# Reordering the scalar engine, the tail pair and the late stores of a vision-transformer layer with CoPE attention and routed experts

## The reference, cut to what matters

```python
h = concat([cls, patches(x) @ W.T + b]) + pos_embed       # 64 images x 37 tokens x 256
# attention: 16 heads of 64, within each image
q, k, v = h @ Wq, split(h @ Wkv)
sim = q @ k.T * scale
P = reverse_cumsum(sigmoid(sim)); P = minimum(P, 63)      # CoPE positions
E = q @ pos_emb                                           # a table of 64 per row
sim = sim + w * E[ceil(P)] + (1 - w) * E[floor(P)]        # w = P - floor(P)
h = layernorm(h + softmax(sim) @ v @ Wout + b_out)
# feed-forward: router takes 2 of 8 experts per token, plus a shared expert
shared = silu(h @ shared_gate) * (h @ shared_up) @ shared_down
routed = sum over 2 experts e: score_e * (silu(h @ gate_e) * (h @ up_e) @ down_e)
out = layernorm(h + shared + routed)
```

## Time and profile before

| what | value |
| --- | --- |
| runs | 741.5 us median of 3 (740.51 to 741.54) |
| the profiled execution | 741.82 us, its span 740.1 us |
| PE busy | 690.8 us, 93% of the span |
| DVE busy | 489.3 us, 66% |
| ACT busy | 418.5 us, 57% |
| the chain that ended last | PE 79%, SP's queue 7%, DMA 5%, ACT 5% |
| granted TensorE clock, mean | 0.98 of full speed |

### The profile page before, as it was taken

One profiled execution on the slowest core, in us unless ns is written; L12 is line 12 of the kernel. 1 busy time (PEld: TensorE's weight loads), 2 busy tenths in 40 slices (PEclk: granted clock), 3 DMA queues, 4 the chain that ended last, 5 costly groups with the idle time before them and its releaser, 6 DMA issues.

```text
span 740.1 us, 14154 instructions
## 1 busy us (share of the span) xinstructions
PE 690.8 (93%) x4720; PEld 590.9 (80%) x4721; DVE 489.3 (66%) x1027; ACT 418.5 (57%) x730; POOL 122.8 (17%) x156
## 2 busy tenths in 40 slices
PE   8996899999999999999999996969799999999996
PEld 5895696969879696969789693848687999999885
DVE  3374687878978787878879787558582222222667
ACT  1653667576676667566675654532215777775363
POOL 2100000000000000000000000000003777775130
PEclk9998999999999999999999999889899999999999
DMA  8720131515141241414131114048003555552811
GB/s 275 207 64 15 37 72 49 97 49 99 54 93 50 66 83 34 95 51 83 54 65 46 36 43 131 23 117 285 21 1 83 136 141 136 142 139 63 277 66 52
DMA packets 85110, 67.17 MB, mean 91 GB/s; under 512 B 51277, under 2 KB 76347, under 8 KB 85079
## 3 DMA queue, kind: packets, MB, share of 16 engines
q1 hardware_dynamic: 80506, 56.73, 29.6%
q0 software_dynamic: 4224, 9.71, 4.4%
q10 hardware_dynamic: 348, 0.34, 0.1%
HBM read 35.60 MB, written 15.75 MB: 69 GB/s over the span
## 4 chain that ended last, share of the span: by engine, by line
PE 79%; SPq 7%; DMA 5%; ACT 5%; issue 3%; DVE 1%; ACTq 0%; DVEq 0%; POOLq 0%
PE ps_S L920 13%; PE ps_S L1408 10%; PE ps_X L1062 8%; PE ps_X L1014 7%; PE ps_S L999 7%; PE ps_S L1138 6%; PE ps_S L1420 5%; PE ps_S L1053 5%; PE ps_S L911 5%; SPq L637 4%; PE ps_S L1341 4%; PE ps_X L920 2%; PE ps_S L929 2%; PE ps_S L1036 1%; SPq L706 1%
## 5 line engine op out<-in xcount | busy, mean ns | idle before, releaser
L1014 PE MATMUL ps_X<-wkv_sb,hT 128*120 128x512 f32 (+1 forms) x176 | 83.1, 604 | 6.3 <-ACT v_sb L1518 6.3
L1408 PEld LDWEIGHTS ps_S<-attnT,v_sb 128*128 128x128 f32 x704 | 84.7, 192 | 4.9 <-ACT attnT L1748 2.8
L1408 PE MATMUL ps_S<-attnT,v_sb 128*128 128x128 f32 x704 | 85.9, 275 | 1.4 <-ACT attnT L1748 1.4
L1901 DVE COPY_PREDICATED table<-bit,table 111x112 f32<-111x112 int16 (+6 forms) x110 | 74.8, 680 | 11.2
L814 POOL TENSOR_TENSOR rs<-ve,neg_half 111x2 f32<-111x2 f32 x11 | 12.2, 1112 | 414.2 <-DVE ve L1987 414.2
L2332 DVE COPY attnT<-ps_S 128x256 f32<-128x256 f32 x44 | 18.7, 424 | 81.1 <-PE ps_S L1420 80.9
L920 PE MATMUL ps_S<-hT,wq_sb 128*128 128x216 f32 (+1 forms) x320 | 62.5, 347 | 5.2 <-ACT kT L1468 5.2
L1014 PEld LDWEIGHTS ps_X<-wkv_sb,hT 128*120 128x120 f32 (+1 forms) x176 | 28.9, 179 | 43.5 <-issue 28.9
L920 PEld LDWEIGHTS ps_S<-hT,wq_sb 128*128 128x128 f32 x320 | 56.4, 188 | 8.3 <-issue 7.0
L1062 PE MATMUL ps_X<-oT,wout_sb 128*128 128x222 f32 x320 | 62.9, 353 | 0.0
L1062 PEld LDWEIGHTS ps_X<-oT,wout_sb 128*128 128x128 f32 x320 | 59.3, 190 | 1.5 <-issue 1.5
(11 more groups left out here) (321 smaller groups left out, 1332.4 us busy)
## 6 DMA issues: line engine op xcount, KB each, us to landing
down_sb<-in_x_dram SPq DMA_DIRECT2D x10, 648.0 KB
gu_sb<-y_d SPq DMA_DIRECT2D x8, 512.0 KB, 6.6
attnT<-attn SPq DMA_DIRECT2D x126, 28.9 KB
h_d<-hT SPq DMA_DIRECT2D x11, 240.0 KB, 2.5
kept<-h_d SPq DMA_DIRECT2D x11, 240.0 KB, 2.7
h_d<-h SPq DMA_DIRECT2D x10, 222.0 KB
attnT<-attn SPq DMA_DIRECT2D x63, 34.7 KB
wkv_sb<-in_L_attn_Wkv_dram SPq DMA_DIRECT2D x2, 1024.0 KB, 12.4
```

Source lines behind the costliest of these rows:

```text
L1014: mm = nc.tensor.matmul(X[:keyed, 1 - s], hT[:, k].rearrange("p b t -> p (b t)")[:, at:at + keyed], wkv_sb[:, k, INNER + 512 * s:INNER + 5 ...
L1408: mm = nc.tensor.matmul(S[:, i, j * FF + f * P:j * FF + f * P + P], held[:, i, k, j, f * P:f * P + P], xgT[:, i, k], start=(k == 0), stop= ...
L1901: A.did(V.copy_predicated(near[:, :, :, 0:SL - d], by_side(bit[:, n], r)[:, :, :, 0:SL - d], near[:, :, :, d:SL]))
```

## The change

- **ACT in every pair:** `values(p,0,1)` and, where `ahead`, `weights(2p-1)` come before `gates(p,0)`.
- **PE in every pair:** the wait for all keys copied moves from ahead of the queries to ahead of their last quarter.
- **Pair 1:** `outputs(0,0)` comes after `score(1,0)` and `values(1,0,1)` and waits for the copies of that score; the score no longer waits for the output copies.
- **Groups 0, 19 and 20:** of the nine placing transfers SP issues six and ACT three, right after its `weights`.
- **The end pair:** chunks 0 to 3 are turned before `outputs(19,1)`, `distance(20)` comes between their copies; the routes of chunks 6, 2, 4 and `by_half` come before `outputs(20,0)`, as do ACT's `logits_out` and `distance(21)`; PSUM banks of turned and routed chunks change.
- **SP's list at the end:** the halves of pair 9 are stored after the first two expert loads, the down loads come last.

The diff, cut:

```diff
+        def to_diagonal(j, b):
+            n, at = in_block[j], from_slot[j]
+            return own_T[PAD * b:PAD * b + PAD, b, at:at + n], turned_attn[PAD * j:PAD * j + PAD, b, :n]
+        def in_two_queues(g):
+            return isinstance(g, int) and (g == 0 or g >= G - 3)
...
+        ROUTES = (0, FULL - 1, 2, 4)
...
@@ SP, place_attn(p, a) @@
-                for j in range(TPG):
-                    n, at = in_block[j], from_slot[j]
+                for j in range(TPG - in_two_queues(g)):
                     for b in range(TPG):
-                        sp.dma_start(own_T[...], turned_attn[...]).then_inc(placed[a], 16)
+                        sp.dma_start(*to_diagonal(j, b)).then_inc(placed[a], 16)
...
@@ SP, end of its list @@
             for t in range(KE):
                 for j, w in enumerate((gate_w, up_w)):
                     sp.dma_start(gu_sb[:, :, t, j, :], ...).then_inc(w_exp, 16)
-            for t in range(KE):
-                sp.dma_start(down_sb[:, :, t, :], ...).then_inc(w_exp, 16)
-            store_halves(G2 - 2)
+                if t == 0:
+                    store_halves(G2 - 2)
...
                 sp.dma_start(hh_d[row:row + r, :], h1_halves[a][:r]).then_inc(hh_stored[a], 16)
+            for t in range(KE):
+                sp.dma_start(down_sb[:, :, t, :], ...).then_inc(w_exp, 16)
...
@@ PE, queries(p, ahead) @@
                     if s == 3 and not next_first(p):
+                        pe.wait_ge(k_sb, p * 4 + 4)
                         outputs(p * 2 - 2, 0)
...
-                        if f > 0:
+                        if f > 0 and not (next_first(p) and a == 0):
                             pe.wait_ge(ot_sb, p * 4 + f // 3 - 4 + 2 * a)
...
@@ PE, pair(p, ahead) @@
                 if next_first(p):
-                    outputs(0, 0)
                     pe.wait_ge(xt_sb, p * 3 + 6)
                     score(p, 0)
                     values(p, 0, 1)
+                    pe.wait_ge(sim_sb, p * 4 + 2)
+                    pe.wait_ge(table_sb, p * 2 + 1)
+                    outputs(0, 0)
...
                     turn_weights(p * 2 - 1, True)
-                    turn(0)
+                    for c in range(2):
+                        turn(c)
                 values(p, 1, 1)
...
-                    pe.wait_ge(h1t_sb, 1)
+                    for c in range(2, 4):
+                        turn(c)
+                    pe.wait_ge(h1t_sb, 4)
                 outputs(p * 2 - 1, 1)
                 score(p, 1)
...
-                    turn(1)
                     pe.wait_ge(ot_sb, p * 4)
                     residual_half(p - 1, X[:, 1], 0)
-                    turn(2)
+                    turn(4)
                     residual_half(p - 1, X[:, 1], 1).then_inc(res_done, 1)
-                    for c in range(3, 5):
-                        turn(c)
+                    turn(5)
+                    turn(6)
                     pe.wait_ge(res_ready, p * KE)
                     route(0)
-                    for c in range(5, FULL):
-                        turn(c)
...
-                if ahead:
-                    pe.wait_ge(k_sb, p * 4 + 8)
-                else:
-                    pe.wait_ge(h1t_sb, FULL)
+                if not ahead:
                     pe.wait_ge(at_sb, 4 * (G - 1))
-                    for j in range(2):
-                        shared_part(0, 0, j)
+                    shared_part(0, 0, 0)
+                    for c in ROUTES[1:]:
+                        route(c)
+                    shared_part(0, 0, 1)
                     shared_part(0, 1, 0)
-                    outputs(p * 2, 0)
-                    pe.wait_ge(ot_sb, 2 * G - 2)
-                    for c in range(2, FULL, 2):
-                        route(c)
-                    shared_part(0, 1, 1)
                     pe.wait_ge(across_sb, FULL + 1)
                     by_half(0, EARLY)
+                    outputs(p * 2, 0)
+                    shared_part(0, 1, 1)
+                    pe.wait_ge(ot_sb, 2 * G - 2)
...
@@ ACT, weights(g, a), behind its two copies @@
+                if in_two_queues(g):
+                    ...
+                    act.wait_ge(at_sb, g * 4 + 4)
+                    for b in range(TPG):
+                        act.dma_start(*to_diagonal(TPG - 1, b)).then_inc(placed[a], 16)
...
@@ ACT, pair(p, ahead, ahead2) @@
                 score(p, 0)
+                if next_first(p):
+                    gates(p, 0)
+                    outputs(0, 0)
                 values(p, 0, 0)
                 if not ahead:
                     softmax_exp(p * 2 - 1)
-                else:
-                    weights(p * 2 - 1)
-                gates(p, 0)
                 values(p, 0, 1)
+                if ahead:
+                    weights(p * 2 - 1, 1)
                 if not next_first(p):
+                    gates(p, 0)
                     split(p - 2)
...
                 else:
-                    weights(p * 2 - 1)
-                    turn(0)
+                    weights(p * 2 - 1, 1)
+                    for c in range(2):
+                        turn(c)
+                    distance(p * 2)
+                    for c in range(2, 4):
+                        turn(c)
                 outputs(p * 2 - 1, 1)
                 for s in range(2):
                     values(p, 1, s)
-                if not ahead:
-                    distance(p * 2)
...
-                    for c in range(1, 3):
+                    turn(4)
+                    softmax_exp(p * 2)
+                    for c in range(5, FULL):
                         turn(c)
-                    softmax_exp(p * 2)
-                    for c in range(3, FULL):
-                        turn(c)
-                    weights(p * 2)
-                    distance(p * 2 + 1)
-                    outputs(p * 2, 0)
+                    weights(p * 2, 0)
...
-            for at, c in enumerate((0, 2, 4, FULL - 1)):
+            for at, c in enumerate(ROUTES):
                 logits_out(c, at)
+                if at == 0:
+                    distance(G - 1)
+            outputs(G - 2, 0)
             softmax_exp(G - 1)
```

More of the change, by code:

```diff
@@ L502, in across_in @@
                 return X[:, 0]
-            return (X[:, 1], S[:, 4], S[:, 5], S[:, 3])[c // 2] if c < FULL else S[:, 4]
+            return (X[:, 1], S[:, 2], S[:, 3], S[:, 4])[c // 2] if c < FULL else S[:, 4]
         kT_flat = kT[:].rearrange("p f a r -> p (f a r)")
@@ L542, in turned_in @@
         def turned_in(c):
-            return X[:, 0] if c >= FULL else (S[:, 4], X[:, 0])[c % 2]
+            if c < 4:
+                return S[:, (4, 5, 2, 3)[c]]
+            return X[:, 0] if c == 5 or c >= FULL else S[:, 4]
         def bank_of(c, f):
@@ L633, in place_attn @@
                 apart(sp)
-                for j in range(TPG):
-                    n, at = in_block[j], from_slot[j]
+                for j in range(TPG - in_two_queues(g)):
                     for b in range(TPG):
-                        sp.dma_start(own_T[PAD * b:PAD * b + PAD, b, at:at + n], turned_attn[PAD * j:PAD * j + PAD, b, :n]
-                                     ).then_inc(placed[a], 16)
+                        sp.dma_start(*to_diagonal(j, b)).then_inc(placed[a], 16)
             def turn_x(p):
@@ L707, in _ @@
                                  ).then_inc(w_exp, 16)
-            for t in range(KE):
-                sp.dma_start(down_sb[:, :, t, :], down_w[:, P * t:P * t + P, :].rearrange("e p n -> p e n")
-                             ).then_inc(w_exp, 16)
-            store_halves(G2 - 2)
+                if t == 0:
+                    store_halves(G2 - 2)
             sp.wait_ge(h1_ready, 2 * G2 + 2)
@@ L719, in _ @@
                 sp.dma_start(hh_d[row:row + r, :], h1_halves[a][:r]).then_inc(hh_stored[a], 16)
+            for t in range(KE):
+                sp.dma_start(down_sb[:, :, t, :], down_w[:, P * t:P * t + P, :].rearrange("e p n -> p e n")
+                             ).then_inc(w_exp, 16)
             for t in range(NT):
@@ L1088, in turn @@
                     pe.wait_ge(table_sb, G - 1)
-                elif c == 1:
-                    pe.wait_ge(v_ready, 2 * G)
-                elif c == 2:
+                elif c == 4:
                     pe.wait_ge(sim_sb, 2 * G)
                     pe.wait_ge(table_sb, G)
-                elif c < FULL:
+                elif c == 5:
+                    pe.wait_ge(v_ready, 2 * G)
+                elif c == FULL - 1:
                     pe.wait_ge(h1t_sb, c - 1)
@@ L1099, in turn @@
                     pe.wait_ge(h1t_sb, c)
-                else:
+                elif c == NEW:
                     pe.wait_ge(h1_ready, 2 * G2 + 2)
@@ L1519, in values, with weights @@
                                ).then_inc(v_ready, 1)
-            def weights(g):
+            def weights(g, a):
                 for j in range(2):
@@ L1526, in weights @@
                                    ).then_inc(at_sb, 2)
+                if in_two_queues(g):
```

(10 more changed lines are left out.)

## The result

The changed kernel takes 718.5 us (median of 4 runs, 717.64 to 720.95) against 741.5 of the kernel before (740.51 to 745.36): ratio 0.969, 95% interval 0.964 to 0.973, or 23.0 us less. Forecast was 718.4. The profiled execution took 717.64 us.

A forecast was written before the change was run, and what follows sets the result against it. The loop was taken as set by a ring of DVE and ACT, with PE's placing stalls costing twice through the lower clock. Terms −0.3 − 3.5 − 5.3 − 7.0 − 7.0 = −23.1 gave 718.4 us; eight in ten, 713 to 728.

The forecast's parts named there:

- Loop: Repeated pairs with ACT's new order and the moved key wait: −0.3 us over eight pairs, pair 2's start included.
- 0.1 − 0.12: about nothing: Per loop pair: gates 0.1 us later, table copy's wait for the score shorter by about 0.12; sum about −0.05.
- Pair 1: Moving `outputs(0,0)` behind score and values starts `outputs(1,1)` at 86.3, −3.1 us; with the key wait −3.5.
- the bound of −0.5: Pair 1: two remaining idle gaps bring the lower clock, slowing `outputs(0,0)` and the score; gain only −0.5 us.
- The bound of −5.7: Pair 1: the gain is −5.7 us if ACT's placing issues cost nothing.
- End pair: Up to `turn_weights(20)`: placing lands earlier, −2.0; clock stays up, −2.85; one turn leaves the path, −0.5; sum −5.3 us.
- `turn_weights(20)` to `(21)`: Tail stretch from the shared parts: moved work fills the placing wait, 18.1 us becomes 11.1, −7.0; bounds −4 to −8.
- Stores: Pair 9's halves stored ahead of most weights: waits go, −4.0, `shared_out(0)` at full clock, −3.0; bounds −7.6 to −3.5.
- A (one issuer): Placing: two queues share one issuer, so nine issues still take 6.8 us; 725 to 728 us, chance 0.12.
- B (gates bind): Loop: value copy and weights delay gates by a full copy, 0.5 us a pair, +4.5: 723 us, chance 0.10.
- C: Stores: halves still come late or ACT lacks room, third stage's wait stays; +4 to +7, 724 us, chance 0.10.
- D: Slower: ACT's issues wait in a busy DMA system while ACT computes nothing; 750 us at 4.23 each, chance 0.04.

The follow-up runs named there:

- placing from SP: Changed kernel with group 0's placing issued by SP alone: 742.02 us (0.9679); with all groups' placing issued by SP alone: 745.65 us (0.9741).
- the tail order back: Changed kernel with routes and `by_half` behind `outputs(20,0)` again, and ACT's `distance(21)` and output copy ahead of the logits: 744.24 us, ratio 0.9736.
- the last two: Changed kernel with unread transpositions filling two tail gaps and group 0 placed by SP: 715.89 us (0.9649); the same plus pair 1's second value half computed twice: 738.52 us (0.9658).

## Why the prediction was right

The sum was −23.1 on the profiled execution and came out at −24.2, the median within 0.1 us of the forecast. The mechanisms held, one of them mis-sized; that the median lies within 0.1 is luck. The terms miss by −2.3 to +0.9, and the profiled execution is the fastest of the four, 0.85 under their median; two of the other three had a lower mean clock (0.992 and 0.993, against 0.995). The terms, each measured by the same marks:

- **Loop, −0.3 predicted, −2.6 measured**: 0.6 up to pair 2's `outputs` (131.13 to 127.22, less pair 1's 3.3) and 2.0 in seven pairs (289.00 to 287.03; 0.59 in the first of them, about 0.23 in each of the other six). This is the step that failed, "0.1 − 0.12: about nothing". The gates slip 0.03 and not 0.1. The key wait gives 0.24 and not 0.12: I read its worth from the bracket, 0.16. But an instruction that waits for nothing starts some 0.09 before the one ahead of it ends (the copy at 195.84, `lg` until 195.93), and that overlap is lost too where it waits. The distance from start to start, 0.93 against 0.69, has both. The first pair's further 0.36 goes with the key wait as well (41.31 us before, 40.72 changed, 41.35 with the wait back); why it is larger there stays open. The bounds of −1 to +4 didn't hold it. That PE's waits are given back to placing was right: PE now waits 0.92 to 0.94 for it.
- **Pair 1, −3.5 predicted, −3.3 measured.** The steps hold one by one: lookup at 65.23 (65.2 said), table copy 70.87 (70.95), `outputs(0,0)` 74.15 (74.15), `outputs(1,1)` 86.20 (86.3). That the lower clock on the score would cost time, as the bound of −0.5 had it, didn't hold: it came in this profile and was hidden. The bound of −5.7, if ACT's issues cost nothing, is what placing from SP gave: −5.9.
- **End pair, −5.3 predicted, −5.4 measured**: `outputs(19,1)` gains 1.85 on `outputs(18,0)` (−2.0 said), the shared part 3.5 more (−3.35 said for clock and turn). In this profile the clock held, as I took it; in five of eight it didn't, and then 1.6 of these 3.5 are lost. That a gap of 2 us leaves the clock up was thus luck in part, and the forecast gives the other case no chance of its own. The residual product is late next, as said (DVE waits 3.98 for it). How much of the clock's share comes from the four turns ahead of `outputs(19,1)` and how much from the two queues is not separated: with one queue and the turns kept PE waited 4.33 us and the clock fell.
- **`turn_weights(20)` to `(21)`, −7.0 predicted, −6.6 measured**, 18.1 to 11.5. PE's 1.80 us of waiting for DVE's norm ahead of it are the exp and the norm that the sum has. But the exp waited 0.55 us for DVE's logits (478.27), where the sum had it wait for the output copy.
- **Stores, −7.0 predicted, −7.3 measured**: `by_half` 4.1 (522.23 − 500.35, less the 17.8 won ahead), then 3.2 by the clock. Alone it was 7.0 by the same marks.
- **Not in the sum:** 0.9 given back at the experts' start, where the first gathered rows come from DMA.

Of the rivals, A (one issuer) falls by the rows above: 4.54 and 2.44 us side by side, 0.75 us an issue on SP. The Trainium skill ("DMA: Bandwidth & Descriptors", Issuing engines are not separate DMA queues) allows the saving of the issuing time and calls it usually small; here it is 3.6 us of 745 in the end pair, where issuing takes three times the landing. B (gates bind) falls by the loop's 6.28. C falls: no wait for halves. D falls: 0.75 to 0.8 us an issue of ACT, behind chunk loads too. But its mechanism, ACT computing nothing while it issues, is real at its true size: it costs 2.6 us in pair 1.

## What to carry to other kernels

A transfer bound by issuing gains from a second queue only where its landing sets the end; the engine that lends the queue stands still for each issue, and what it would have computed is late. Price a removed wait by the start-to-start distance of the two instructions, with and without it, not by the idle time in the bracket. Count a wait of a few us on TensorE twice only with a chance beside it, and where the clock matters fill it with work that needs nothing.

## What the runs showed of the hardware

- The same gap of 2.1 us on PE costs the clock in some profiles of the same kernel (0.65) and not in others (1.00). The Trainium skill ("TensorE: Matmul & The Clock Gate", Part 1: The HAM clock gate) says of the rise at the start of a kernel that its time differs from run to run; these traces show such a difference for the fall behind a gap in the middle. In pair 1 the score behind a wait of 2.94 to 3.03 us took 2.30 us in three profiles and 3.04 to 3.79 in four; behind the 3.08 us of the tail order back the clock held. Behind the waits of 3.81 to 8.20 us, ten of them between 45 us and the experts' start in these profiles, it was lower every time. With the gaps filled none of three profiles fell in the tail; that is few, against five in eight.
- Chips differ by 3% on this program, all in one stage: up to the experts' start the traces agree, behind it 175 to 178 us on one kind and 197 to 201 on the other. There PE waits 16.8 us ahead of the gate and up products and not 2.3, 10.4 of it for ACT's copy of the gathered rows, and these products take 3.5 us more. What is slower on these chips isn't shown.
- Not tried: the changed kernel and the last two on one chip together; the four turns put back behind `outputs(19,1)`; a third queue for placing.
